# A vision tower on one core: who issues the attention weight loads of the patch embedding, and where the first tokens are split

## The reference

```python
patches = _patchify(images, PATCH)
emb = jnp.einsum('bnk,kd->bnd', patches, W_proj) + b_proj
h = emb + pos_table[None, :, :]
q = jnp.einsum('bsd,hde->bshe', h, W_Q) + b_Q     # 192 x 768, as are K and V
...
h = _layernorm(h + attn_out)
```

## Time and profile before

| | us |
|---|---|
| median of 3 runs | 906.39 |
| lowest, highest | 905.71, 907.11 |
| profiled execution, its own time | 909.75 |
| its span in the profile | 908.0 |
| PE, DVE, ACT, POOL busy | 831.0, 543.1, 461.0, 410.3 |

### The profile page before, as it was taken

How to read it: one execution, slowest core, us unless ns; L and a number is a source line. 1 busy time by engine, 2 the same in 40 slices (tenths; PEclk the granted TensorE clock), 3 DMA queues, 4 the chain that set the end, 5 groups by cost and what they waited for, 6 DMA issues and landing times. The chain is left out here.

```text
span 908.0 us, 20892 instructions
## 1 busy us (share of the span) xinstructions
PE 831.0 (92%) x7511; PEld 748.5 (82%) x7511; DVE 543.1 (60%) x1466; ACT 461.0 (51%) x1150; POOL 410.3 (45%) x489
## 2 busy tenths in 40 slices
PE   9899999999998798998999988988979999999982
PEld 8889998899997577776999986776757899899972
DVE  2236555556665788884773326888875622466645
ACT  0346565555644587874345526877735221255533
POOL 1535444344444444432441225777851355244445
PEclk9989999999999999996999998999969999999997
DMA  9810111111110131214400002633200011233243
GB/s 315 255 50 21 22 35 37 31 31 30 38 36 2 33 67 25 37 19 123 74 1 1 1 26 42 138 68 68 42 7 2 29 62 63 76 103 100 83 149 116
DMA packets 103940, 55.75 MB, mean 61 GB/s; under 512 B 67264, under 2 KB 94512, under 8 KB 103840
## 3 DMA queue, kind: packets, MB, share of 16 engines
q1 hardware_dynamic: 98032, 43.04, 19.9%
q0 software_dynamic: 3792, 7.84, 2.5%
q10 hardware_dynamic: 2016, 3.54, 1.3%
HBM read 29.81 MB, written 13.97 MB: 48 GB/s over the span
## 5 line engine op out<-in xcount | busy, mean ns | idle before, releaser
L931 POOL TENSOR_TENSOR attn_prob<-attn_prob,attn_recip 100x432 f32<-100x432 f32 x64 | 58.6, 915 | 75.5 <-DVE attn_recip L1310 75.2
L450 POOL TENSOR_TENSOR attn_prob_x<-attn_prob,attn_recip 100x864 f32<-100x864 f32 x32 | 52.7, 1646 | 52.7 <-DVE attn_recip L759 52.7
L1886 POOL DMA_INDIRECT results<-moe_hid_shared x43 | 41.3, 960 | 58.4 <-ACT moe_hid_shared L2101 58.4
L1596 ACT ACTIVATE mlp_hid<-psum,columns 128x384 f32<-128x384 f32 x72 | 38.1, 579 | 41.4 <-PE psum L96 41.4
L1060 PEld LDWEIGHTS psum<-attn_prob_t,attn_values 108*64 108x64 f32 x1024 | 39.3, 142 | 13.6 <-ACT attn_prob_t L1179 7.8
L1060 PE MATMUL psum<-attn_prob_t,attn_values 108*64 108x36 f32 x1024 | 41.6, 228 | 6.1 <-ACT attn_prob_t L1179 4.1
L2076 ACT ACTIVATE moe_silu<-psum 128x384 f32<-128x384 f32 x36 | 17.7, 491 | 56.6 <-PE psum L107 56.6
L1033 PE MATMUL psum<-attn_keys_a,attn_q_a 128*64 128x288 f32 x256 | 45.8, 437 | 0.0
L1043 PE MATMUL psum<-ident,attn_prob 100*108 100x100 f32 x256 | 35.8, 265 | 9.5 <-POOL attn_prob L931 9.5
L1172 ACT ACTIVATE attn_prob<-attn_prob 100x432 f32<-100x432 f32 x64 | 36.5, 571 | 15.5 <-POOL attn_prob L938 14.7
L1305 DVE TENSOR_REDUCE attn_row_sum<-attn_prob 100x12 f32<-100x432 f32 x64 | 38.0, 594 | 8.1 <-ACT attn_prob L1172 7.9
(11 more groups left out here) (473 smaller groups left out, 2853.5 us busy)
## 6 DMA issues: line engine op xcount, KB each, us to landing
embed_patches<-in_x SPq DMA_DIRECT2D x8, 768.0 KB, 17.2
sorted_rows<-mlp_pad_zeros SPq DMA_DIRECT2D x1, 4214.0 KB, 15.7
moe_hid_shared<-sorted_rows SPq DMA_DIRECT2D x43, 98.0 KB, 2.0
attn_v<-attn_v_tok SPq DMA_DIRECT2D x16, 216.0 KB
attn_values<-attn_v_tok SPq DMA_DIRECT2D x96, 27.0 KB
side_raw_a<-in_w_gu_dram SPq DMA_DIRECT2D x8, 288.0 KB, 3.3
side_raw_b<-in_w_gu_dram SPq DMA_DIRECT2D x16, 144.0 KB, 3.4
h_rows<-results SPq DMA_DIRECT2D x6, 288.0 KB, 5.3
```

Of the source, the lines that this page charges most:

```text
L450: nc.gpsimd.tensor_tensor(prob_x[k % 2][:, :, :, :], prob[k % 3][:, :, :].rearrange("p h (a n) -> p h a n", a=1) .to_broadcast([QP, HEADS, ...
L931: nc.gpsimd.tensor_tensor(pr, pr, recip[k % 2][:, :].rearrange("p (h a) -> p h a", a=1) .to_broadcast([QP, HEADS, SEQ]), ALU.mult).then_in ...
L1596: nc.scalar.activation(hid_step(n), bank(n % 3)[:, 0:MW], ACT.Gelu, bias=b_up[:, c:c + 1]).then_inc(S["gelu_done"], 1)
L1886: nc.gpsimd.indirect_dma_start(out=results, out_offset=bass.IndirectOffsetOnAxis(ap=x_in[j % x_ring][:, D:D + 1].bitcast(U32), axis=0), in ...
```

## The change

SP issues the four weight jobs, each between patch batches: job 0 behind batch 5, job 1 behind batch 6, job 2 behind batch 7, and job 3 (with its wait for job 0's remainders) behind batch 8 and `columns`, ahead of batch 9. The third part of the position table goes behind batch 6 instead of ahead of it. ACT keeps only the rounding and no longer waits for patch batches. DVE splits the first tokens after tile 15 instead of after tile 16, and scales the columns after tile 16 instead of after tile 17.

```diff
             load(5)
+            load_one(sp, S, stage_a, stage_b, jobs, 0)
+            load(6)
             load_pos(2, 6)
-            load(6)
+            load_one(sp, S, stage_a, stage_b, jobs, 1)
+            load(7)
+            load_one(sp, S, stage_a, stage_b, jobs, 2)
+            load(8)
             prep["load_columns"](sp)
-            for n in range(7, len(batches)):
-                load(n)
+            load_one(sp, S, stage_a, stage_b, jobs, 3)
+            load(9)
             prep["load"](sp)
...
+                if t == NT - 3:
+                    following.split(dve, S)
                 if t == NT - 2:
-                    following.split(dve, S)
-            prep["scale_columns"](dve)
+                    prep["scale_columns"](dve)
...
-            batch_landed(act, 3)
-            load_one(act, S, stage_a, stage_b, jobs, 0)
-            round_one(nc, act, S, stage_a, stage_b, jobs, 0)
-            batch_landed(act, 6)
-            load_one(act, S, stage_a, stage_b, jobs, 1)
-            batch_landed(act, 7)
-            load_one(act, S, stage_a, stage_b, jobs, 2)
-            round_one(nc, act, S, stage_a, stage_b, jobs, 1)
-            round_one(nc, act, S, stage_a, stage_b, jobs, 2)
-            batch_landed(act, 8)
-            load_one(act, S, stage_a, stage_b, jobs, 3)
+            for j in range(3):
+                round_one(nc, act, S, stage_a, stage_b, jobs, j)
             following.round(act, S)
             round_one(nc, act, S, stage_a, stage_b, jobs, 3)
```

## The result

The changed kernel is faster by 0.3%: a median of 904.99 us in 20 executions (898.33 to 907.97) against 907.22 in 20 of the kernel before (905.06 to 910.87), ratio 0.9968 with a 95% interval of 0.9953 to 0.9984. That is 1.5 to 4.3 us of gain where 5.5 was forecast, and 904.99 lies above the range, whose upper end was 903.8. Two later comparisons, of 12 executions each, gave 0.9965 (0.9945 to 0.9986) and 0.9975 (0.9953 to 0.9996). The changed kernel also scatters more: over all 44 executions its times have a standard deviation of 2.7 us, those of the kernel before, over 110, one of 1.7.

The account below looks back on a forecast made before the run. The embedding's end was taken to be bound by job 3's late load, ACT and POOL, with PE waiting. Gains of 3.2 us (earlier barrier) and 2.3 us (clock) made 5.5: 906.4 - 5.5 = 900.9 us, range 899.5 to 903.8.

Parts of the forecast that it names:

- What bounds the kernel: End of the embedding: job 3's late load, then ACT, then POOL set the stage's end; PE waited 4.64 us.
- my line: Embedding loads summed as one sequence behind the same DMA engines: job 3.0 us, batch 1.96, job 3 landing at 36.6.
- Part 1, when the loads land: Embedding loads: batch 7 just in time, batches 8 and 9 late by 0.4 and 0.3; PE ends 0.7 us later.
- The starved rival: Embedding: whole jobs between batches make PE wait; gain 3.6 us, time 902.8, or 905.1 if the clock falls; chance 0.07.
- part 2: End of the embedding: ACT, POOL and SP no longer last, barrier 43.4 instead of 46.6; 3.2 us, between 1.3 and 3.9.
- Part 3, the clock: After the embedding's barrier: clock stays up, projections to the next line take 8.4 us instead of 10.7; gain 2.3 us.
- The DVE part: Last embedding tiles: moving the split of the first tokens earlier on DVE is worth 0.3 us at the last tile.
- the clock falls anyway: At the embedding's barrier: 0.8 us of idle and earlier stalls lower the clock; gain 3.2, time 903.2; chance 0.13.
- SP's wait holds up batch 9: Embedding loads: SP waits for job 0's remainders until 38.1, stage ends 2.7 us later, time 909.1; chance 0.03.
- the issuing engine does not matter: Embedding loads: transfers share the same engines, job 3 lands at 42.6 whoever issues it, time 906.4; chance 0.03.

Follow-up runs that it names:

- The doubled rows: Weight rows 128 to 191 laid out twice, so both stage_b halves load as one transfer: in the changed kernel ratio 0.9931, in the kernel before 0.9947.
- the batches ahead: The changed kernel with each weight job loaded behind its patch batch instead of ahead of it: ratios to the kernel before 0.9974 and 0.9958.
- second profile of the relative: Repeat of the changed kernel with each weight job behind its patch batch, no edit: barrier at 46.92 us, ratio to the kernel before 0.9958.

## Why the prediction was wrong

**What bounds the kernel: right.** The stage ended with the chain of job 3, ACT and POOL, and the change took it off the end: POOL at 42.16 instead of 46.25 (40.2 was forecast; job 3 landed 2.0 us later than in my line).

**Part 1, when the loads land: the step that failed.** "Batch 7 is just in time, batch 8 is 0.4 us late, batch 9 then another 0.3": PE's waits for patches were 1.7 to 2.3 us in three profiles, and the stall 2.0 to 2.4 with what its weight loads waited for batch 9. It is a term that was mis-sized. My line took 3.0 us for a job and 1.96 us for a batch behind it, 4.96 together. Job 1 to job 2 took 5.7 (5.6 and 5.4 in the other two profiles). In the first profile the job itself was near (25.0 to 28.2 for job 1, 30.8 to 33.9 for job 2: 3.3 and 3.1 us), but the batch behind it took 2.6 us (28.2 to 30.8 and 33.9 to 36.5). In the other two the jobs took 3.2 to 3.5 us and the batches 2.3 to 2.4, so the excess is shared between them. The start was late too, by 0.3 to 0.6 us: 24.96, 24.73 and 24.66 for the third position part. With those terms batch 8 landed at 36.48, not 34.2. I had taken 1.96 us from a stretch at the full rate, and put the whole price of the half-width transfers on the job. The doubled rows show that the loss belongs to the way those halves are loaded: when they come as one transfer the pair takes 3.9 us, the 2 x 1.96 of my own full rate. Why part of the price lands on the batch behind, and not on the job, was not settled.

My range for the stall had 2.6 us as its upper end, but only 0.07 of the chances stood on it, while 0.70 stood on a stall of 0.7 us or less. The starved rival is what happened in the milder form: the barrier came 1.3, 1.3 and 1.9 us sooner than the 46.60 of before, and 1.3 was the lowest value of part 2.

**Part 3, the clock: right in kind, high in size.** It stayed at 1.00 across the barrier in every profile of the changed kernel, and from the first projection to L524 it took 8.5 us (8.4 forecast), with the small wait for the key copy (0.2 us). But the 2.3 us came from one profile of before; three give 1.8 on average.

**The DVE part:** 0.3 us, as forecast, but that is luck: I had it from the split, and in the changed kernel it came from the columns, which without the move stand behind the last addition. With the batches ahead the moved columns held up the last addition instead.

**The sum.** By the profiles: barrier 46.5 (three with the old issue order) to 45.1 (three of the changed kernel), 1.4 us; clock 1.8; together 3.2 instead of 5.5. Measured, by the three ratios: (1 - 0.9968) x 907.2 = 2.9, then 3.2 and 2.3 us. That closes within the intervals. Of the 2.3 us that are missing from the 5.5, 1.8 belong to the barrier (part 1) and 0.5 to the clock (part 3). The time, 904.99, is 4.1 above my 900.9: 2.3 by these two, 0.8 because the kernel before had a median of 907.22 here and not 906.39, and the remaining 1.0 because the medians differ by only 2.2 us, which is within the scatter. The wider scatter of the changed kernel goes with the mean clock; that slower transfers bring it about, as in the second profile of the relative, was only argued, and the spread with the rows doubled speaks against it.

**The rivals.** That the clock falls anyway was not seen at the barrier. That SP's wait holds up batch 9 was wrong: it ended at 26.40. That the issuing engine does not matter was wrong for this change, since job 3 landed 4.1 us sooner. With the rows doubled it holds for the barrier: 43.31 with ACT issuing, 43.35 with SP.

**The range** was too narrow at the top because it took in little of the starved case, and also because it was built around one execution: 0.7 us was allowed for the scatter of the runs, from three of them. The changed kernel's first 20 executions scatter over 9.6 us.

## What to carry to other kernels

When loads are put into one line, price each by the rate at which its own shape runs, and allow for the one behind it too: here a pair of loads over half the partitions each took about the time of one full-width load of twice their bytes, and the batch behind was late as well. Before reordering such loads, ask whether they can be given the full width. Here that alone made the next stage 5.5 us earlier at L524, the change under study alone 3.5, and the change on top of it nothing. When executions of one kernel scatter by more than the gain, judge the total by many of them and by their mean clock, and read a profile only up to the point where all profiles still agree.

## What the runs showed of the hardware that was not expected

- The same program (batches ahead of jobs) had its last weight job land at 38.81 in one execution and at 42.20 in another, with the DMA engines fully busy in both (303 and 290 GB/s from 24 to 38 us).
- After idle stretches of PE of the same length (4.64 to 4.71 us) the clock was at 0.50 for 5.9 us in two executions and for 3.2 us in a third.
- Filling such an idle stretch with 14 matmuls of a constant tile kept the clock at 1.00, and the next ten microseconds became 1.0 to 2.35 us shorter, by which profile without them it is compared with.
- Two small DVE operations took 1.31 and 1.44 us instead of 0.16 and 0.23 when they ran beside POOL's remainders, and each ended within 0.03 us of one of them.
- Loads of the same bytes moved 393 GB/s instead of 292, at the same busy share of the DMA engines (1.04), once two transfers over 64 partitions had become one over 128.
